# Fused attention and expert layers, two deep: eight moves of work in the first and last slots of the closing attention stage

## The reference

```
x = x + L0_xattn(layernorm(x), ctx)     # 16 heads, rotary embedding, output projection
x = x + L0_ffn(layernorm(x))            # 16 experts, top 2 of them, and a shared network
x = x + L1_xattn(layernorm(x), ctx)
x = x + L1_ffn(layernorm(x))

L1_xattn: q = x @ Wq.T; k, v = ctx @ Wk.T, ctx @ Wv.T   # 32 heads of 8, k and v interleaved
          q, k = rmsnorm(q), rmsnorm(k)                 # over the 8 values of a head
          out = softmax(q k^T / sqrt(8)) v              # no output projection
L1_ffn:   h = silu(x @ rw1.T + rb1)                     # router, 64 wide
          logits = (h @ rw2.T + rb2)[:, :16] + gates
          coeff = softmax of the 2 largest logits, 0 elsewhere
          wxa = (x @ A) * coeff                         # 16 experts of rank 16: 256 wide
          out = x @ W.T + bias + wxa @ B
```

## Time and profile before

| | |
|---|---|
| median of 3 runs | 370.22 us (368.12, 370.22, 371.21) |
| the profiled execution | 370.5 us |
| its span on the core | 368.8 us |
| mean granted TensorE clock in it | 0.912 |
| TensorE busy | 294.5 us, 80% of the span |
| VectorE busy | 264.8 us, 72% |
| ScalarE busy | 185.2 us, 50% |
| GpSimd busy | 113.3 us, 31% |
| second attention stage | about 260 to 334 us of the span |

### The profile page before, as it was taken

How to read it: one execution, slowest core, us unless ns; L and a number is a source line. 1 busy time by engine, 2 the same in 40 slices (tenths; PEclk the granted TensorE clock), 3 DMA queues, 4 the chain that set the end, 5 groups by cost and what they waited for, 6 DMA issues and landing times.

```text
span 368.8 us, 7376 instructions
## 1 busy us (share of the span) xinstructions
PE 294.5 (80%) x2676; PEld 182.9 (50%) x2676; DVE 264.8 (72%) x675; ACT 185.2 (50%) x334; POOL 113.3 (31%) x224
## 2 busy tenths in 40 slices
PE   4337878888887776899995998966878888969796
PEld 3212344344343332487684986853544555544364
DVE  6967889889898896678943454527478888678872
ACT  1111465665756657625441677623557778743211
POOL 1134364463543222161771112057400000202300
PEclk9955799999999999969997899995599999987899
DMA  7594269478684202300226366946445766300002
GB/s 242 168 270 115 88 173 285 134 219 262 170 261 132 73 23 74 111 2 1 101 100 188 125 230 230 331 136 192 130 138 164 228 181 175 102 2 1 0 30 85
DMA packets 68435, 52.29 MB, mean 142 GB/s; under 512 B 4784, under 2 KB 65200, under 8 KB 68400
## 3 DMA queue, kind: packets, MB, share of 16 engines
q1 hardware_dynamic: 62768, 40.84, 36.8%
q10 hardware_dynamic: 4096, 6.79, 5.8%
q0 software_dynamic: 1536, 4.20, 3.6%
HBM read 30.38 MB, written 21.23 MB: 140 GB/s over the span
## 4 chain that ended last, share of the span: by engine, by line
PE 42%; DVE 29%; POOL 8%; issue 8%; DMA 6%; ACT 5%; SPq 2%; DVEq 0%; POOLq 0%
DVE mx L1749 10%; PE psum L1112 5%; PE psum L747 4%; POOL sorted_x L1647 4%; PE psum L997 4%; PE psum L1125 4%; PE psum L783 4%; POOL low L1651 3%; PE psum L732 3%; PE psum L1088 3%; PE psum L768 2%; PE psum L874 2%; ACT prob L1251 2%; PE psum L1215 2%; DVE rope_ab L1738 2%
## 5 line engine op out<-in xcount | busy, mean ns | idle before, releaser
L1749 DVE TENSOR_REDUCE mx<-psum 128x2 f32<-128x512 f32 x128 | 81.1, 684 | 16.0 <-PE psum L747 15.4
L1251 ACT ACTIVATE prob<-psum 128x1024 f32<-128x1024 f32 x64 | 64.5, 1023 | 37.6 <-PE psum L768 37.3
L747 PE MATMUL psum<-kstk,qstk 64*128 64x256 bf16 x256 | 27.4, 296 | 26.3 <-DVE mx L1749 15.0
L783 PE MATMUL psum<-prob,vt 128*32 128x256 f32 x512 | 34.3, 385 | 6.2 <-ACT prob L1251 5.1
L1474 ACT ACTIVATE prob<-psum 128x1024 f32<-128x1024 f32 x32 | 32.5, 1023 | 0.2 <-PE psum L1072 0.2
L747 PEld LDWEIGHTS psum<-kstk,qstk 64*128 64x128 bf16 x256 | 8.7, 97 | 43.1 <-DVE mx L1749 28.7
L542 POOL TENSOR_TENSOR parts<-qk_rest,parts 128x256 bf16<-128x256 f32 (+1 forms) x15 | 13.8, 920 | 51.3 <-ACT parts L1411 47.7
L1088 PE MATMUL psum<-prob,vt 128*32 128x128 f32 x512 | 21.9, 292 | 5.4 <-ACT prob L1474 5.3
L768 PE MATMUL psum<-qstk,kstk 64*128 64x256 bf16 x256 | 24.9, 279 | 0.8 <-DMA qstk<-mT 0.8
L783 PEld LDWEIGHTS psum<-prob,vt 128*32 128x32 f32 x512 | 13.9, 109 | 18.5 <-ACT prob L1251 7.4
L1258 ACT CAST parts<-qk 128x512 bf16<-128x512 f32 x8 | 4.9, 618 | 31.4 <-POOL qk L536 16.8
(11 more groups left out here) (281 smaller groups left out, 624.6 us busy)
## 6 DMA issues: line engine op xcount, KB each, us to landing
qstk<-stack_scratch SPq DMA_DIRECT2D x30, 256.0 KB, 3.8
stack_scratch<-parts SPq DMA_DIRECT2D x22, 192.0 KB, 2.1
kstk<-key_scratch SPq DMA_DIRECT2D x16, 256.0 KB, 3.8
kstk<-stack_scratch SPq DMA_DIRECT2D x14, 256.0 KB, 5.8
stack_scratch<-parts SPq DMA_DIRECT2D x24, 128.0 KB, 2.1
low<-in_wup ACTq DMA_DIRECT2D x4, 640.0 KB, 4.5
wdn<-in_wdn ACTq DMA_DIRECT2D x4, 640.0 KB, 5.8
prob<-sorted_x SPq DMA_DIRECT2D x8, 256.0 KB, 4.2
```

Of the source, the lines that this page charges most:

```text
L747: last = nc.tensor.matmul(banks[s][:, nb * D:(nb + 1) * D], qstk[par][rows, pair, nb * P:(nb + 1) * P], kstk[par][rows, pair, :], start=Tr ...
L783: last = nc.tensor.matmul(pv_bank(1)[32 * j:32 * j + 32, g * D:(g + 1) * D], vt[b % 2][:, mb, 4 * t + j, 8:40] if low else vt[b % 2][:, mb ...
L1251: nc.scalar.activation(prob[(b * PAIRS + k) % 3][:], exp_buf(k).rearrange("p a n -> p (a n)"), ACT.Exp, scale=SCALE).then_inc(exp_done, 1)
L1749: nc.vector.tensor_reduce(mx[:, half, :, 4 * s + p4:4 * s + p4 + 1], bank.rearrange("n (b m) -> n b m", b=2), AX_X, ALU.max).then_inc(misc ...
```

## The change

Eight edits, all of order; no operation is added or taken away.

1. The `v` use of block 1 moves from spot 0 to spot 4 of the first slot; VectorE's copy of it moves too.
2. On ScalarE in the first slot, `guess_roots(2)` moves behind the fourth exponential, and the cast of the first part of block 2 behind the first exponential of block 1.
3. On VectorE, adding experts and centring block 3 moves from behind block 2's sum of squares to the prologue, next to block 2's centring.
4. On VectorE, at spot 4 of block 6, the statistics of blocks 4 and 5 stand ahead of `silu(0)`.
5. `wide(1)` and `dlg(0)` change places (spots 1 and 3 of block 7). ScalarE copies wide(1) one step earlier and takes the exponential of the gap one step later.
6. `weights_of(0)` moves from spot 4 of block 7 to between silu(1) and silu(2).
7. `wide(4)` moves from behind dh(2) to right behind `wide(3)`.
8. GpSimd's bias sum for block 4, and those for 5 to 7 queued behind it, waits for the third silu.

```
--- before.py
+++ after.py
@@ -443,14 +443,14 @@
 
 
         D_EARLY = {(5, 7): [("dxT", 0), ("dxT", 1)], (6, 1): [("dxT", 2), ("dxT", 3)], (6, 3): [("wide", 0)],
-                   (6, 5): [("dh", 0)], (7, 1): [("dlg", 0)], (7, 3): [("wide", 1)], (7, 5): [("dxT", 4), ("dxT", 5)],
+                   (6, 5): [("dh", 0)], (7, 1): [("wide", 1)], (7, 3): [("dlg", 0)], (7, 5): [("dxT", 4), ("dxT", 5)],
                    (7, 7): [("wide", 2)]}
 
         def c_uses(b, spot):
 
-            u = [("v", b + 1)] if spot == 0 and b + 1 < NB else []
+            u = [("v", b + 1)] if spot == 0 and 0 < b < NB - 1 else []
             if b == 0:
-                u += {1: [("xT", 2)], 3: [("q", 2)], 6: [("qT", 2)]}.get(spot, [])
+                u += {1: [("xT", 2)], 3: [("q", 2)], 4: [("v", 1)], 6: [("qT", 2)]}.get(spot, [])
             u += [("qT", b + 2)] if spot == 3 and 0 < b < NB - 2 else []
             u += [("o", b - 1)] if spot == 4 and b else []
             u += [("xT", b + 3)] if spot == 5 and b + 3 < NB else []
@@ -1219,11 +1219,11 @@
             ring("o", 7)
             pe.wait_ge(exp_done, NB * (PAIRS + C_STEPS) + 1)
             wide(3)
+            wide(4)
             ring("dxT", 6)
             ring("dh", 1)
             ring("dxT", 7)
             ring("dh", 2)
-            wide(4)
             ring("dlg", 1)
             pe.wait_ge(pv_free, 3 * NB + 2)
             flip_wxa(0)
@@ -1475,6 +1475,7 @@
                                          scale=SCALE).then_inc(exp_done, 1)
                     if k == 0:
                         if b == 1:
+                            first_parts_c(full("qT", 2), bank_of("qT", 2), 0, 0)
                             second_parts_c(gone_v("qT", 2), 0)
                         if 0 < b < NB - 2:
                             squares(b + 2, full("q", b + 2), bank_of("q", b + 2))
@@ -1490,23 +1491,22 @@
                         if b == 6:
                             take_dxT(2)
                             take_dxT(3)
+                        if b == 7:
+                            take_wide(1)
                         if b == 0 and by_act(("xT", 2)):
                             take_xT_c(2)
                     if k == 2:
                         if b == 0:
                             squares(2, full("q", 2), bank_of("q", 2))
-                            guess_roots(2)
                         if b == 5:
                             guess_ln(0, 0, 4)
                         if 0 < b < NB - 2:
                             first_parts_c(full("qT", b + 2), bank_of("qT", b + 2), b % 2, (b + 1) // 2)
-                        if b >= 6:
-                            take_wide(b - 6)
-                        if b == 7:
-                            gap_exp(0)
+                        if b == 6:
+                            take_wide(0)
                     if k == 3:
                         if b == 0:
-                            first_parts_c(full("qT", 2), bank_of("qT", 2), 0, 0)
+                            guess_roots(2)
                         elif b < NB - 2:
                             second_parts_c(gone_v("qT", b + 2), b % 2)
                         if b + 3 < NB and by_act(("xT", b + 3)):
@@ -1516,6 +1516,7 @@
                         if b == 7:
                             take_dxT(4)
                             take_dxT(5)
+                            gap_exp(0)
                             take_wide(2)
 
 
@@ -1673,6 +1674,8 @@
 
             for b in range(NB):
                 pool.wait_ge(xn_ready, 3 * NB + b + 1)
+                if b == 4:
+                    pool.wait_ge(silu_done, 3)
                 last = nc.gpsimd.tensor_tensor(xall[:, b, :], xall[:, b, :], rows[:, 4 * NE:4 * NE + D], ALU.add)
                 if b < N_RAW:
                     steps.then(last)
@@ -2078,10 +2081,10 @@
                                           ).then_inc(misc_free, 1)
                 elif kind == "q":
                     sum_squares(b)
-                    if b < 7:
+                    if 2 < b < 7:
                         attend_norm(b + 1, 1)
                         center(b + 1, (b + 1) % 2)
-                    else:
+                    elif b == 7:
                         dve.wait_ge(misc_free, gone_v("o", 3))
                         ln_stats(0, 4)
                     scale_queries(b, bank)
@@ -2157,6 +2160,8 @@
             c_pro(("qT", 1))
             attend_norm(2, 1, added=True)
             center(2, 0)
+            attend_norm(3, 1)
+            center(3, 1)
 
             def filled(*use):
                 dve.wait_ge(misc_full, full(*use))
@@ -2244,12 +2249,10 @@
                     if b == 5 and spot == 4:
                         ln_normalize(2)
                         ln_normalize(3)
-                    if b == 7 and spot == 4:
-                        weights_of(0)
                     if b == 6 and spot == 4:
-                        silu(0)
                         dve.wait_ge(misc_free, gone_v("o", 5))
                         ln_stats(4, 2)
+                        silu(0)
 
 
             def weigh(b):
@@ -2280,6 +2283,7 @@
             ln_roots(3, 7, 1)
             ln_normalize(7)
             silu(1)
+            weights_of(0)
             silu(2)
             weigh(0)
             weigh(1)
```

26 lines of the change are left out of this document (12 added, 14 removed).

## The result

The changed kernel took 373.89 us (median of 4 runs, 372.98 to 377.81) where the kernel before took 370.22. The ratio is 1.0128, 95% interval 1.0081 to 1.0175. The same kernel run again gave 373.59 us and a ratio of 1.0103 (1.0057 to 1.0149). It is about 1% slower. 372.4 was forecast, in a range of 368.5 to 375.0: the sign and the place were right, the size was 1.5 us too small. The span of the profiled execution grew from 368.8 to 371.2 us, by 2.4; the forecast sum was 2.3.

The account below looks back on a forecast made before the run. The prediction took VectorE's chain to bound the attention blocks, with TensorE holes costing idle time and half clock behind them. Terms -0.35 + 0.1 + 2.4 + 0.2 made about +2.3, forecast 372.4 us, range 368.5 to 375.0.

Parts of the forecast that it names:

- First slot: Block 0 of the last attention stage: three edits together gain 0.35 us, between +0.3 and -1.45.
- query projection: In block 0 of the last attention stage: starts at 265.4, takes about 2.0 us at half clock, ends at 267.4.
- the walk: Engine-by-engine path through block 0 of the last attention stage: scaling ends at about 270.6, pvT at about 273.2.
- Last pvT: VectorE's last transpose in the last attention stage: starts at 335.65 instead of 338.14, -2.5 us.
- sign of being wrong: At the end of attention: VectorE's final pvT not 2 us earlier would mean an unseen wait holds the queue.
- the end: After attention: logits +0.1 us, logits through two deltas +2.4, GpSimd's delayed additions +0.2.
- the first hole: TensorE nearly empty from 330.75 to 334.6, about 3.4 us; the clock falls and wide(2) takes 3.8 us.
- The gain spent: From final pvT to logits: the 2.5 us are spent by block 6's transposes at 343.5; logits at 350.0, +0.1.
- The second hole: TensorE empty from 346 to 350 before the second logits; logits through two deltas then take 5.9 us, +2.4.
- The late sums: GpSimd's four additions land at 350 to 353: 0.2 us taken, up to 2.0; about 1.4 freed at 342 to 344.
- slower by over 1%: Whole kernel: outcome more than 3.7 us slower, chance 0.20.
- a change within 1%: Whole kernel: outcome less than 3.7 us from the time before, counted as no change, chance 0.75.

Follow-up runs that it names:

- Idle products: Changed kernel plus three products whose results nobody reads, between the last router hidden and the second logits: 372.17 us, ratio 1.0034 to the kernel before.
- wide(4) late: Changed kernel with the wide product of block 4 back behind the second router hidden: 370.23 us, ratio 1.0002 to the kernel before.
- sums at the third sigmoid: Kernel with TensorE's gaps filled by its own wide products, but bias sums from block 4 on waiting for the third sigmoid: 365.42 us, ratio 0.9875.
- holes filled: Changed kernel with wide(3) to wide(7) placed in TensorE's gaps, first weights at spot 4, bias sums early: 365.37 us, ratio 0.9871 to the kernel before.

## Why the prediction was right

**First slot: direction right, size too small.** -0.35 forecast, -0.83 measured. From the profile after:

```profile
260.35 0.61 PE L1072 MATMUL psum<-qstk,kstk 64*128 64x128 bf16 x8
...
265.99 1.53 PE L1041 MATMUL psum<-wc,xT 128*128 128x256 f32 x4
```

```profile
269.77 0.25 DVE L2071 SCALAR_TENSOR_TENSOR rs<-ss,eps_v,guess 128x32 f32<-128x32 f32 x1 [1.28 <-ACT guess L1399]
...
273.28 0.70 DVE L2106 STREAM_TRANSPOSE pvT<-psum 128x512 f32<-128x512 f32 x1
```

The mis-sized term is the query projection: I took 2.0 us, since it would stay at half clock; it took 1.53, because the clock rose within it as before (1.40). The scaling starts at 269.77 (root) and ends at 270.70; less the 0.56 by which this execution is later, it and all behind it come 0.5 earlier than in the walk. pvT comes 12.93 us after the first scores, where it came 13.75 us after them.

**Last pvT: -2.5 forecast, -1.2 measured.** The prediction had named this as a sign of being wrong: a last pvT that is not 2 us earlier. By that sign the path up to it was wrong, though the time came out in the range. VectorE, then GpSimd:

```profile
328.36 0.43 DVE L2182 TENSOR_TENSOR rs_a<-ln_v,ln_g 128x2 f32<-128x2 f32 x1
328.83 0.65 DVE L2183 SCALAR_TENSOR_TENSOR rstd<-rs_a,ln_g 128x2 f32<-128x2 f32 x1
...
334.68 0.42 DVE L2102 TENSOR_TENSOR xall<-psum,xall 128x256 f32<-128x256 f32 x1
336.93 0.72 DVE L2106 STREAM_TRANSPOSE pvT<-psum 128x512 f32<-128x512 f32 x1 [1.83 <-PE psum L1088]
...
349.35 1.28 DVE L2267 TENSOR_TENSOR wxa<-prob,comb 128x256 f32<-128x256 f32 x2
...
351.98 0.68 DVE L1892 TENSOR_TENSOR hot_t<-sel_s,top 128x64 f32<-128x64 f32 x1
...
368.65 0.42 DVE L2274 TENSOR_TENSOR xall<-psum,xall 128x256 f32<-128x256 f32 x1 [0.44 <-PE psum L1215]
```

```profile
328.05 0.73 POOL L1683 TENSOR_TENSOR xall<-xall,prob 128x256 f32<-128x256 f32 x1 [4.97 <-ACT prob L1454]
328.73 0.73 POOL L1679 TENSOR_TENSOR xall<-xall,rows 128x256 f32<-128x256 f32 x1
...
349.57 3.01 POOL L1679 TENSOR_TENSOR xall<-xall,rows 128x256 f32<-128x256 f32 x4 [7.79 <-DVE eh L2201]
```

Two things were missed. GpSimd's addition of block 1's wide product (328.05) and block 2's bias sum queued behind it (328.73) now lie beside the roots, because wide(1) is copied earlier: the two steps take 0.43 and 0.65 us where they took 0.12 and 0.16, 0.8 together. I had counted the additions at the end only. And the clock was down already at the second pair of transposes and the last product (335.15 and 335.77: 0.69 and 1.08, where full clock takes 0.44 and 0.64), not only behind them: 0.7 more. In turn it rose within wide(2): 2.82, not 3.8. Both sums end at the same place: I had wide(2) done at 339.4, and the output's transposes start at 339.44. That is luck: a late start and a short product cancelled. In the eight profiles with the first hole open wide(2) took 2.78 to 3.10 us in five and 3.78 in three.

**The gain spent.** Block 6's transposes were forecast at 343.5 and came at 343.10 (343.52 before). The logits were forecast at 350.0 and came at 349.57 (349.82 before). VectorE is 1.2 us earlier at the last pvT, and 0.25 of it arrives at the logits, less than the 0.28 by which the whole slot starts earlier.

**The second hole**: forecast 346 to 350, measured 345.67 to 349.57; logits to the end of the second delta 5.9 forecast, 6.21 measured; clock 0.50 from 349.5 on. The stretch grew 1.76 times, for which I had taken 1.7. The Trainium skill, TensorE: Matmul & The Clock Gate, Terms, prices a stretch at half of its length: 3.1 of 6.21. The trace has 2.69 (6.21 less 3.52), between my 2.4 and that.

**The late sums**: the prediction misread here. The three additions from 341.14 are for blocks 3, 4 and 5, and edit 8 holds only those from block 4 on. Block 3's is still at 341.06 after the change and slows VectorE's first root step (341.07, 0.73 us), so 0.8 us come free at the normalizing and not 1.4; it made no difference, since wide(3) and wide(4) hold TensorE until 343.10. The four held additions (3.01 us from 349.57) lie beside the weighings and the picks, as forecast; 1.28 and 0.68 us where the trace of before has 0.75 and 0.23, 1.0 us in all. On the path it cost nothing, since wide(5) and wide(6) hold TensorE until the flips at 359.21; I had 0.2. In a kernel without that cover it costs 0.57 and what the clock makes of it (above).

**The sum** of the spans (2.3 and 2.4) agrees for partly cancelling reasons: the first slot 0.5 better, the end 0.3 worse, and 0.56 us from ahead of the edited part in the one profile. (The terms add up to 2.35 and give 372.6 on the median, not 372.4.) The medians moved by 3.7, and by 3.6 the second time, more than the 2.4 of the profiles. So what was measured, 1.0 to 1.3% slower, falls on the edge of what the prediction called "slower by over 1%", with a chance of 0.20, and not among its 0.75 for a change within 1%. The mean clocks say where to look: 0.907 over 81 executions of the kernel before, 0.9035 over six of the changed one, yet 0.912 in the profile of before and 0.903 in that of after. As an estimate, the time at half speed is twice the missing share times the time: 0.093 x 2 x 370 = 69 us before, 0.0965 x 2 x 373.6 = 72 after. In which stretches the others fell I can't say, since a timed execution leaves no rows.

## What to carry to other kernels

Before a move, look at what the engine that is left behind does in the meantime. Here two products were taken out of the places where they bridged TensorE's waits, in order to be early where nobody waited for them; the wait stayed and the engine came out of it at half clock, so the loss was larger than the work moved. Order filler work by the gaps it closes, and look at all of them at once: one gap filled with what bridged the next was no gain here. A delay on VectorE costs nothing where TensorE's queue ends last (the late sums in the changed kernel), and more than itself where it opens a gap: 0.57 us became 1.98 in the filled one.

## What was new about the hardware

- Idle products made a program faster: three of them, 2.84 us of TensorE's time, gave 2 us of the tail and 0.7 to 0.9% of the time back.
- A gap of 2.00 us (wide(4) late) and one of 1.97 (sums at the third sigmoid) were each followed by half clock in their profiles, while gaps of 1.14 (idle products), 1.39 and 1.40 (holes filled) were not. In the kernel before, two gaps of 1.50 and 1.41 with sixteen short instructions between them were too; the earlier trace rows has a part of them.
- The length of the gap alone does not tell. In the kernel before, gaps of 1.30, 0.27 and 0.55 us ahead of block 6's and 7's transposes and hidden layer were followed by half clock (wide(4), 3.25 us); in the kernel with the holes filled, gaps of 1.41, 0.27 and 0.55 at the same place were not (wide(6), 1.98). And the clock need not fall in the gap: behind those of 2.00 and 1.97 us it fell about 1.8 and 1.7 us after TensorE was at work again.
- A small VectorE step with two SBUF inputs beside a GpSimd addition of two SBUF tensors took 0.40 to 0.73 us instead of 0.12 to 0.23. The Trainium skill, SBUF — State Buffer, Who interferes with whom, says that such a pair contends for a shared port that only one of them holds at a time; the rows agree.
